# Where TensorE transposes the second half's probabilities: ahead of, or behind, the second feed-forward product

## What is computed

```
def _layer(x, wqkv, qs, ksc, wo, lg, lb, w1, b1, w2, b2):
    h = shift_token(x)
    q, k, v = split(h @ wqkv)                  # 8 heads of 64
    q, k = rotary_xpos(l2norm(q) * qs, l2norm(k) * ksc)
    o = local_attention(q, k, v)               # windows of 128, each looks at itself and the one before
    x = x + o @ wo
    h = layernorm(shift_token(x)) * lg + lb
    a, g = split(h @ w1 + b1)                  # 682 each
    return x + (a * gelu(g)) @ w2 + b2
for l in range(2):
    x = _layer(x, ...)
```

## Time and profile before

| | |
|---|---|
| three runs | 4319.83, 4322.89, 4324.39 us (median 4322.89) |
| the profiled execution | 4329.71 us, of which the span is 4327.9 |
| PE busy over the span | 4001.2 us (92%), weight loads 3306.8 (76%) |
| DVE | 3055.6 us (71%) |
| ACT | 2852.8 us (66%) |
| POOL | 2198.8 us (51%) |
| TensorE's granted clock, mean | 0.986 of 2.4 GHz |

### The profile page before, as it was taken

The page is one execution under the profiler, slowest core; times in us unless marked ns, Lnnn a source line. Parts: engine busy times, 40 slices in busy tenths (PEclk is TensorE's granted clock), DMA queues, the critical chain, the costliest instruction groups (busy, mean ns, idle before and its releaser), DMA issues.

```text
span 4327.9 us, 96690 instructions
## 1 busy us (share of the span) xinstructions
PE 4001.2 (92%) x36356; PEld 3306.8 (76%) x36416; DVE 3055.6 (71%) x7412; ACT 2852.8 (66%) x7273; POOL 2198.8 (51%) x2168
## 2 busy tenths in 40 slices
PE   5999999999999769999999999999999999999997
PEld 3777777777777557888888888877888888888886
DVE  3888888888888756666666666666667666666664
ACT  3666666666666456677676767766766676666665
POOL 3888888988888823333333333333333333333332
PEclk8999999999999989999999999999999999999999
DMA  5453444434444010000000000000000000000000
GB/s 103 69 74 63 60 69 70 68 63 66 68 70 59 28 45 12 20 16 16 19 17 14 17 19 16 16 27 13 26 21 21 27 21 21 22 26 24 19 24 24
DMA packets 175047, 159.22 MB, mean 37 GB/s; under 512 B 22175, under 2 KB 173558, under 8 KB 174582
## 3 DMA queue, kind: packets, MB, share of 16 engines
q1 hardware_dynamic: 174582, 153.04, 19.1%
HBM read 52.31 MB, written 25.17 MB: 18 GB/s over the span
## 4 chain that ended last, share of the span: by engine, by line
PE 16%; issue 15%; ACT 15%; DVE 14%; POOL 5%; SPq 0%; DMA 0%; POOLq 0%; DVEq 0%; ACTq 0%
PE b_X L1439 4%; PE b_S L1459 3%; DVE b_S L1251 3%; PE b_M L1561 3%; ACT b_p L1199 3%; ACT b_hn L1083 2%; ACT L1167 2%; PE b_M L1552 2%; DVE b_ss L1225 2%; DVE b_qT L1240 2%; ACT b_g L1167 2%; DVE b_kT L1240 2%; POOL b_rstd L1041 1%; PE b_F L1588 1%; PE b_S L1469 1%
## 5 line engine op out<-in xcount | busy, mean ns | idle before, releaser
L251 POOL TENSOR_TENSOR a_z<-a_p 128x1024 f32<-128x1024 f32 x256 | 604.0, 2359 | 187.4 <-ACT a_p L338 184.9
L1199 ACT ACTIVATE b_p<-b_S,b_nb 128x256 f32<-128x256 f32 (+1 forms) x1024 | 444.5, 446 | 328.8 <-DVE b_nb L1251 328.8
L338 ACT ACTIVATE a_p<-a_S 128x512 f32<-128x512 f32 x1024 | 528.7, 602 | 191.3 <-PE a_S L528 189.5
L1439 PE MATMUL b_X<-b_wqkv,b_hT 128*128 128x512 f32 x2304 | 651.5, 419 | 1.3 <-DVE b_hT L1275 1.3
L1508 PE MATMUL b_F<-b_hnT,b_w 128*114 128x256 f32 (+1 forms) x4608 | 628.8, 286 | 5.7 <-issue 5.7
L1508 PEld LDWEIGHTS b_F<-b_hnT,b_w 128*114 128x114 f32 (+1 forms) x4608 | 573.6, 177 | 19.0 <-issue 6.1
L1439 PEld LDWEIGHTS b_X<-b_wqkv,b_hT 128*128 128x128 f32 x2304 | 418.1, 190 | 101.2 <-issue 21.8
L977 POOL TENSOR_TENSOR b_t<-b_t 128x512 f32<-128x512 f32 x128 | 165.1, 1290 | 633.8 <-DVE b_t L1223 633.8
L422 DVE TENSOR_TENSOR a_p<-a_p,a_O 128x1536 f32<-128x1536 f32 x256 | 447.2, 1747 | 5.4 <-ACT a_O L315 3.8
L1588 PE MATMUL b_F<-w_w,b_a 114*128 114x256 f32 (+1 forms) x1536 | 365.4, 388 | 69.4 <-DVE b_a L879 68.8
L1260 DVE TENSOR_SCALAR b_a<-b_F,w_b 114x256 f32<-114x256 f32 (+1 forms) x384 | 183.8, 479 | 340.9 <-ACT b_g L1110 340.8
(11 more groups left out here) (152 smaller groups left out, 8719.7 us busy)
## 6 DMA issues: line engine op xcount, KB each, us to landing
a_q<-a_parts SPq DMA_DIRECT2D x256, 128.0 KB, 5.0
a_k<-a_parts SPq DMA_DIRECT2D x256, 128.0 KB, 5.0
a_x<-in_x SPq DMA_DIRECT2D x16, 512.0 KB, 3.9
a_xr<-in_x SPq DMA_DIRECT2D x64, 128.0 KB, 5.2
x_after_heads<-a_n SPq DMA_DIRECT2D x64, 128.0 KB, 5.4
b_x<-x_after_heads SPq DMA_DIRECT2D x16, 512.0 KB, 4.1
x_after_layer<-b_xo SPq DMA_DIRECT2D x32, 256.0 KB, 2.8
b_x<-x_after_layer SPq DMA_DIRECT2D x16, 512.0 KB, 4.1
```

Of the source, the lines that this page charges most:

```text
L251: nc.gpsimd.tensor_tensor(z8[:], e[:, 0:8], e[:, 8:16], ALU.add).then_inc(s_zt, 1)
L338: nc.scalar.activation(probs[u % NE][:, hs], S[:, hs], ACT.Exp, scale=HDIM ** -0.5).then_inc(s_exp, 1)
L1199: last = nc.scalar.activation(probs[hf][:, i, keys(w_)], SB[:, i, keys(w_)], ACT.Exp, bias=nb[hf][:, i:i + 1], scale=-1.0, accum_out=rs[w_ ...
L1439: last = nc.tensor.matmul(X[i][:], hT_of(k, a), wqkv[:, b, k, i * INNER:(i + 1) * INNER], start=(k == 0 and (a, b) == PART_PAIRS[0]), stop ...
```

## The change

Two lines move. `transpose_probs(T, w_, 1)` is issued ahead of the second feed-forward product, behind the third hidden block:

```
                 if feed:
                     hidden(T, 2, w_, layer)
+                if live:
+                    transpose_probs(T, w_, 1)
                 h, d, m = output_half(n, w_)
                 if seq_exists(m):
                     t = w_ % 2
...
                     last.then_inc(s_w2, 1)
-                if live:
-                    transpose_probs(T, w_, 1)
```

## The result

The changed kernel takes 4425.94 us (median of four runs, 4423.78 to 4429.48) against 4323.08 for the kernel before (four runs, 4319.83 to 4324.39): a ratio of 1.024, 95% interval 1.0222 to 1.0258. It is 103 us slower. The forecast was 4432, its range 4393 to 4456. The profiled execution of the changed kernel took 4423.78 us.

The account below looks back on a forecast made before the run. TensorE sets the pace, busy 1236 of 1305 us of the second stage. Tile-end delays of 78 us plus 31 for clock falls give 109 on 4322.9: 4432 us, range 4393 to 4456.

Parts of the forecast that it names:

- The bare wait: At tile ends TensorE would idle for the exponentials before the transposes: 2.17 us at w_ = 2, 1.26 at 1 and 3.
- The slack behind each end: Next tile's scores hide delay only as far as they already waited; 3.03 us a sequence remain, 2.33 from n = 18.
- w_ = 2 0.96 - 0.43 = 0.53: End of w_ = 2, n = 18 to 31: TensorE's 0.96 us delay less the next scores' 0.43 wait leaves 0.53.
- w_ = 1 and 3 0.90 each: Ends of w_ = 1 and 3: 1.26 us delay less the scores' old wait of 0.36 leaves 0.90 a tile.
- The clock: TensorE's granted clock falls behind some of the 30 gaps of 2.17 us at w_ = 2, 1.7 us each: 31 us.
- The six in ten: Assumed share of the 30 gaps at w_ = 2 followed by a clock fall; three of four early gaps had one.
- The rival by which the clock stays up: All delays at the tile ends, no clock falls: 4322.9 + 78 = 4401 us; chance 0.26.
- Dips at w_ = 0 and 1 as well: Sign that the forecast is wrong: TensorE's clock also falls at the ends of w_ = 0 and 1.
- the rival of 4470: Clock falls after all 30 gaps of 2.17 us and the 1.72 of w_ = 0 in n = 18 to 31; chance 0.07.
- The faster rival: Gating's wait at the product hides under the transposes if probabilities come in time: some 35 us gained, 4288; chance 0.03.
- 0.5 to 1: Microseconds the next scores take back of about 2 us gained per sequence if the gating's wait vanishes.

Follow-up runs that it names:

- the three parts of the change: Transposes moved ahead of the product only at w_ = 2, only at 1 and 3, only at 0, each against the kernel before: 4354.06, 4374.67, 4328.47 us.
- the filled gap: Against the changed kernel, four more products into bank F1 ahead of the transposes at w_ = 2: 4391.37 us.
- clearing the head: Against the kernel before, query and key copies go ahead of the layernorm's rows on ScalarE, and TensorE transposes those rows behind the scores: 4242.54 us.

## Why the prediction was right

**The bare wait: right, shown.** "In every kind of tile the probabilities come later than both the hidden block and the gating." The gaps are 2.14 us for 2.17 forecast at w_ = 2, 1.09 for 1.26 at w_ = 1 and 3, and at w_ = 0 1.33 for 1.35, from n = 18 on 1.71 for 1.72. The product waits three times instead of 64, and VectorE waits for it at L1359, 114 times. Once the falls are counted, the three parts of the change add up to its whole cost to within some 1 us, less than the intervals of the runs can tell.

**The slack behind each end: right in kind, one term mis-sized.** The sum gave 3.03 us for a sequence up to n = 17 and 2.33 behind; 2.86 and 2.01 were measured. Three of the four tiles of the second form agree to 0.02. The step that was off is "w_ = 2 0.96 - 0.43 = 0.53" in n = 18 to 31, the slack behind w_ = 2: the table has it in the tile that follows, w_ = 3, which should grow by 0.83 and grew by 0.54. ("w_ = 1 and 3 0.90 each" held: their move alone leaves 0.88.) I had counted only the wait that stands at the scores, 0.43 in the earlier trace rows. TensorE lost time at the rows' transposes (L1421) too, ahead of which no wait is listed there: in the kernel before, L1417 and L1421 of that tile start 0.44 us apart, at most other heads 0.22. The same two rows before, and then in the changed kernel, where they are 0.22 apart:

```profile
3647.34 0.38 PE L1417 MATMUL b_X<-c_ident,b_x 128*128 128x128 f32 x2
3647.78 0.44 PE L1421 MATMUL b_X<-c_ident,b_hn 128*128 128x128 f32 x2
...
3721.89 0.38 PE L1417 MATMUL b_X<-c_ident,b_x 128*128 128x128 f32 x2
3722.11 0.38 PE L1421 MATMUL b_X<-c_ident,b_hn 128*128 128x128 f32 x2
```

So that time was slack as well, and the change uses it up. From the first L1533 of this tile to its scores it takes 4.62 us before and 3.85 in the changed kernel: 0.77 given back, as in the move at w_ = 2 alone (0.78). Of these 0.43 are the listed wait, 0.22 stand ahead of L1421, and 0.12 in no list. With the 1.31 that the end of w_ = 3 costs by itself, for 1.26, that leaves the 0.54.

In all the delays came to 68 us instead of 78: 4.5 from n = 18 to 31, 2.7 from n = 2 to 17; tile 4, the first of n = 1, is 1.5 shorter, which I didn't foresee: the fall at its head in the kernel before (0.72 from 1615 to 1621 us in the earlier trace rows) did not come in the changed kernel, so this is the clock and no delay. The tiles behind the two splits make up the rest.

**The clock: the size right, the count nearly, the idea of chance wrong.** "30 x 0.6 x 1.7 = 31 us." A fall costs 1.68, and 20 of 30 gaps had one: 34 us, and the filled gap gives 35 back. The six in ten came from four gaps, and the count was luck to that extent: the same gaps in the kernel with w_ = 2 alone fell in 11 of 30. They also are not scattered: fourteen sequences in a row (n = 2 to 15), then from n = 18 on every second one. The rival by which the clock stays up, 4401, fell: gaps of 2.14 us were enough in 20 of 30 cases. The kernel with the filled gap is that rival built: 4391, 10 less than 4401, as the delays were too large by 10. The Trainium skill, page "TensorE: Matmul & The Clock Gate", section "Why this matters for your kernels", allows longer idle gaps than these; the trace does not agree. "Dips at w_ = 0 and 1 as well", the rival of 4470, did not come, not even behind the gaps of up to 1.7.

**The faster rival fell twice.** The probabilities do not come in time, and the wait that the change hides was worth nothing in this kernel. The prediction put it at some 35 us if the probabilities were early; the gating on GpSimdE shows 0 for 55 us of removed waits, since the next tile's head took them back whole, not "0.5 to 1" of two.

**The sum.** 68 for 78 and 34 for 31 leave 102 for 109, and 4426 for 4432. The two errors have opposite signs, so the total is a little better than its parts.

## What to carry to other kernels

Before an operation is moved ahead of one that waits, look at what it will wait for itself: an in-order engine that has something to do while another engine finishes should keep that work in front, even if it begins with a short wait. A delay costs only what the slack behind it doesn't cover, and a wait that is removed gains only if no wait stands behind it; both are read at the next tile's head, and clearing the head first (here 79 us) is what made the removal at the product worth anything (15.5 us of 56). Where a new gap of some 2 us remains, a few products into a bank that is free can keep the clock up; here they cost nothing (tiles of 22.97 us for 22.98) and gave 35 us.

## What the runs showed of the hardware

- Gaps of the same size, with the same work around them, are sometimes followed by 3.4 us at 1.2 GHz and sometimes not: 2.18 us without and 2.19 us with, a sequence apart. In the changed kernel all of n = 2 to 15 fell, and from n = 18 on every second; with w_ = 2 alone, 11 of the 30 did. It is regular, so where in time the gap lies seems to matter; what sets it stays open. No gap of 1.1 to 1.7 us ahead of these transposes was followed by a fall in n = 2 to 31.
- TensorE can lose time at an instruction without a wait on the list: at a tile's head about 0.1 us more than the listed wait came back when the wait was removed (6.48 to 6.04 us with a wait of 0.36), and 0.22 us that stood ahead of the rows' transposes in n = 24 were gone in the changed kernel.
